# Neighbour codes before attention's set-up, and attention's end and statistics inside a selection, in a two-layer graph kernel

## What is computed

```python
# layer 0: h = relu(layernorm(x))
scores = where(A != 0, -arange(N), -inf)
vals, idx = top_k(scores, 25)              # the first 25 neighbours of each node
agg = X[idx].max(axis=2)                   # largest feature over them; relu of it if degree <= 25
x = x + relu(concat([X, agg]) @ W + b)
# layer 1: h = relu(layernorm(x))
hidden = h @ W.T
attn = leaky_relu(attn1[:, :, None] + attn2[:, None, :], 0.2)   # attn1, attn2 = hidden @ a
attn = softmax(where(mask > 0, attn, attn - 1e12))
x = x + attn @ hidden + bias
```

## Time and profile before

| what | value |
|---|---|
| runs, us | 5257.32, 5246.94, 5260.84 (median 5257.32) |
| profiled execution | 5242.94 us, its span 5241.1 us |
| POOL busy | 3058.9 us (58%), 3204 instructions |
| PE busy | 2621.3 us (50%) |
| DVE busy | 2599.8 us (50%) |
| ACT busy | 1563.8 us (30%) |
| granted TensorE clock, mean | 0.71 |

### The profile page before, as it was taken

The page is one execution under the profiler, slowest core; times in us unless marked ns, Lnnn a source line. Parts: engine busy times, 40 slices in busy tenths (PEclk is TensorE's granted clock), DMA queues, the critical chain, the costliest instruction groups (busy, mean ns, idle before and its releaser), DMA issues.

```text
span 5241.1 us, 38278 instructions
## 1 busy us (share of the span) xinstructions
PE 2621.3 (50%) x8782; PEld 1593.0 (30%) x8782; DVE 2599.8 (50%) x6725; ACT 1563.8 (30%) x1745; POOL 3058.9 (58%) x3204
## 2 busy tenths in 40 slices
PE   2122234556455555545555545555655555555479
PEld 1011112333233333323333323333323333332256
DVE  5444454455464455455445545445455554554442
ACT  3011122233332323333223333232333322333135
POOL 5565556566665666666666566665666665656520
PEclk8555557777676777666777767776766777766699
DMA  6354446556555566565555555656556665555320
GB/s 252 114 163 143 143 140 183 156 184 177 174 170 181 161 187 178 173 187 173 178 164 180 172 179 172 184 163 185 174 175 188 178 183 153 173 172 159 118 91 29
DMA packets 477228, 866.03 MB, mean 165 GB/s; under 512 B 308298, under 2 KB 309204, under 8 KB 456660
## 3 DMA queue, kind: packets, MB, share of 16 engines
q0 software_dynamic: 153600, 419.64, 27.8%
q1 hardware_dynamic: 305140, 378.64, 22.6%
q10 hardware_dynamic: 18432, 67.12, 3.5%
HBM read 690.98 MB, written 119.54 MB: 155 GB/s over the span
## 4 chain that ended last, share of the span: by engine, by line
PE 24%; DVE 23%; another core or an unknown queue 21%; issue 19%; ACT 10%; SPq 1%; DMA 1%; POOL 1%; ACTq 1%; DVEq 0%; POOLq 0%
PE acc L1331 13%; DVE highest L915 6%; ACT nm_t L566 4%; DVE lin L939 3%; DVE top L849 2%; DVE key L855 2%; PE bank L1264 2%; ACT wgt L602 2%; PE pen L1324 2%; PE pen L1323 1%; DVE stat L776 1%; PE bank L1244 1%; ACT pen L596 1%; POOL near L521 1%
## 5 line engine op out<-in xcount | busy, mean ns | idle before, releaser
L521 POOL DMA_INDIRECT near<-table_dram,idx x3200 | 3058.7, 956 | 1958.4 <-issue 990.5
L1331 PE MATMUL acc<-hid,wgt 128*128 (+1 forms) x4096 | 1163.2, 435 | 494.9 <-ACT wgt L602 431.4
L1331 PEld LDWEIGHTS acc<-hid,wgt 128*128 128x128 f32 x4096 | 873.6, 219 | 685.9 <-issue 427.4
L915 DVE TENSOR_TENSOR highest<-near,highest 128x512 f32<-128x512 f32 x1280 | 889.8, 695 | 142.6 <-DVE highest L915 65.2
L931 DVE SCALAR_TENSOR_TENSOR x_q<-bank,x_q 128x256 f32<-128x256 f32 x128 | 54.1, 423 | 1194.2 <-PE bank L1266 1038.3
L602 ACT ACTIVATE wgt<-pen,a_slope 128x512 f32<-128x512 f32 x448 | 304.7, 680 | 910.1 <-remote 576.3
L1264 PE MATMUL bank<-w_sb,h_t 128*128 128x256 f32 x1024 | 381.3, 537 | 334.1 <-ACT h_t L692 263.1
L566 ACT ACTIVATE nm_t<-adj_i,big_c 128x2048 bf16<-128x2048 int32 x128 | 498.0, 3941 | 4.9 <-DMA adj_i<-in_adj_dram 4.9
L1273 PE MATMUL acc<-cst,wgt 128*128 128x128 f32 x248 | 61.0, 427 | 812.1 <-ACT wgt L577 779.8
L939 DVE CUSTOM_DVE_ANT_0 lin<-acc,nm_q 128x2048 bf16<-128x2048 f32 x108 | 247.4, 2291 | 376.6 <-ACT acc L713 364.8
L849 DVE MAX8 top<-key 128x8 f32<-128x256 f32 (+1 forms) x1024 | 355.2, 386 | 127.6 <-remote 92.5
(11 more groups left out here) (148 smaller groups left out, 2172.4 us busy)
## 6 DMA issues: line engine op xcount, KB each, us to landing
adj_i<-in_adj_dram SPq DMA_DIRECT2D x128, 1024.0 KB
nmask_dram<-nm_t ACTq DMA_DIRECT2D x128, 512.0 KB
nm_q<-nmask_dram SPq DMA_DIRECT2D x29, 2048.0 KB
near<-table_dram,idx POOLq DMA_INDIRECT x3200
h_q<-table_dram SPq DMA_DIRECT2D x32, 512.0 KB
x_q<-in_x_dram SPq DMA_DIRECT2D x32, 512.0 KB
xmid_dram<-x_q SPq DMA_DIRECT2D x32, 512.0 KB
o_q<-xmid_dram SPq DMA_DIRECT2D x32, 512.0 KB
```

Source lines behind the costliest of these rows:

```text
L521: pool.indirect_dma_start(out=near[:, t % 2, k, :], out_offset=None, in_=table, in_offset=bass.IndirectOffsetOnAxis(ap=idx[:, t, k:k + 1], ...
L915: nc.vector.tensor_tensor(highest[:, :], pair(k), highest[:, :], ALU.max).then_inc(mx_step, 1)
L1331: mm = nc.tensor.matmul(acc[:, t, 0:C + 1], wgt_part(j)[:, t * P:(t + 1) * P], hid[:, bass.ds(batch * NJ + j, 1), 0:C + 1].rearrange("p a ...
```

## The change

It has two parts. In the first, PE packs the words of the next quad's first pair right behind layer 0 of tile 0, ahead of attention's set-up, and DVE makes the codes from them ahead of the maximum of tile 1. In the second, DVE's end of attention and the statistics stand between the two halves of the second pair's selection, behind the residual of tile 3, and no longer behind that selection.

```diff
--- before.py
+++ after.py
@@ -1154,7 +1154,6 @@
 
                 def selected(pair, between):
                     if "index" in stages:
-                        index_words(s + 1, pair)
                         index_rest(pair, between)
                     else:
                         between()
@@ -1162,11 +1161,20 @@
                 def third_tile():
                     finished(1)
                     gathered(2)
+
+                def quad_end():
+                    finished(3)
+                    if "attend" in stages:
+                        attend_end(a)
+                    if "gather" in stages:
+                        statistics_of_step(s, stages)
 
                 gathered(0)
                 if "attend" in stages:
                     attend_setup(a, lo)
                 finished(0)
+                if "index" in stages:
+                    index_words(s + 1, 0)
                 gathered(1)
                 selected(0, third_tile)
                 finished(2)
@@ -1174,13 +1182,9 @@
                     index_words(s + 1, 1)
                 gathered(3)
                 if "index" in stages:
-                    index_rest(1, lambda: finished(3))
+                    index_rest(1, quad_end)
                 else:
-                    finished(3)
-                if "attend" in stages:
-                    attend_end(a)
-                if "gather" in stages:
-                    statistics_of_step(s, stages)
+                    quad_end()
 
             b2.start(-1, -1)
 
@@ -1417,10 +1421,10 @@
                 if "project" in stages:
                     project(s - 1)
                 gathered(0)
+                if "index" in stages:
+                    index_prep(s + 1, 0)
                 if "attend" in stages:
                     attend_setup(a)
-                if "index" in stages:
-                    index_prep(s + 1, 0)
                 gathered(1)
                 for c in range(8):
                     if "attend" in stages:
```

## The result

| | before | after |
|---|---|---|
| median, us | 5252.13 (5237.10 to 5260.84, 4 runs) | 5336.70 (5323.85 to 5345.69, 4 runs) |
| profiled span, us | 5241.1 | 5340.6 |
| granted TensorE clock, mean | 0.71 | 0.70 |

The ratio is 1.0156, with a 95% interval of 1.0126 to 1.0186: 84.6 us slower. The forecast was 5345 in a range of 5180 to 5440.

The account below looks back on a forecast made before the run. Bound: one step's chain across engines, stretched by long POOL gather runs, not POOL alone. 3.0 us in 27 steps (81) plus 12 on 5242.94 gave 5336; plain runs' median is 14 us higher, so 5345, range 5180 to 5440.

Parts of the forecast that it names:

- Front half: Codes and index matmuls ahead of tile 1's maximum: a cost between 3.1 and 4.4 us a step, taken as 4.0.
- it ends at 2632.3, 4.4 us later: Tile 1's maximum starts 4.7 us later, falls wholly into POOL's slow stretch and so ends 4.4 us later.
- Two of my own signs: POOL's pause at `agg_made` near 9 us; forecast wrong if the second maximum ends less than 3 us later.
- a half sentence: Next POOL pauses end after POOL stops and carry its lateness on to the engines; reason for taking 4.0 us.
- Back half: Reciprocal and statistics right behind tile 3's residual: 4.7 us gained, less the front's 4.0; both branches still slower, 3.0 a step.
- the first branch: A hop (DVE to ACT or ACT to POOL) is held up and POOL stops at `h2_made`: 2.5 us slower.
- `project`'s start: If POOL stops at `h2_made`, `project` starts between 1 and 4 us later than before, taken as 2.5.
- L939's idle time: 13.3 us of cover for the moved rounds, used up if POOL passes `h2_made`; L939 then starts 3.5 us later.
- the steps without attention: Four steps where DVE waits for index matmuls held by ACT's masks: 0 to 9 us lost, 3 a step, 12 total.
- Codes late by 7.3 us: Rival: L1244's message to DVE is held up 7.3 us, 10.3 us a step lost, 5533 us; chance 0.14.
- The chain simply gets shorter: Rival: statistics end fast and the long run hurts nothing behind; 3.5 us a step faster, 5150 us; chance 0.24.
- Nothing measurable: Rival: front and back cancel (4.0 against 4.7), POOL's pauses absorb the rest; 5243 to 5270 us; chance 0.12.

Follow-up runs that it names:

- the kernel without pauses: Kernel before, with POOL's three waits at (1, 4), (1, 9) and (1, 21) left out: 5656.41 us, ratio 1.073.
- Part 1 alone: Kernel before plus only the words and codes moved ahead of attention's set-up, the statistics left behind the selection: 5345.31 us, ratio 1.0126.
- the early pause: POOL's wait for `out_made` moved from (1, 4) to (0, 23): changed kernel 5310.65 us, ratio 1.007; with only the second part of the change 5245.38 us, 0.996.
- the first trace: First profiled execution of the unchanged kernel, the one the prediction read: period 154.9 us, profiled span 5241.1 us.
- the control: Kernel before, unchanged, executed once more with the experiments: 5266.46 us, ratio 0.9995.
- part 2 alone: Kernel before plus only attention's end and statistics moved inside the second pair's selection: 5281.25 us, ratio 1.0009; with `out_made`'s wait also at (0, 23), 0.996.
- a second one: Changed kernel with `out_made`'s wait at (0, 23) and also the wait for tile 1's maximum moved from (2, 16) to (2, 18): 5220.62 us, ratio 0.9943.

## Why the prediction was right, and where it was off

**The mechanism.** That long POOL runs stretch what lies in them is shown: by two steps of one execution (7.9 against 19.5 us), by the kernel without pauses (32.8 us), and by moving one wait (L623 4.85 us behind its matmuls, then 0.15). Instructions themselves do not get longer, they start late: on DVE, operations of 0.17 us came 0.7 or 1.4 us apart inside the run and 0.2 us apart behind the stop; L623 started 5.2 us behind PE's matmuls. With half the bytes the held stretch was as long, so it is not the bytes. POOL's issuing or the number of gathers is left, and these runs don't part the two; nor do they show through what path it acts, or that DVE's late starts and ACT's have the same cause.

By the rule of the Trainium skill's page SBUF — State Buffer, section Who interferes with whom, only DVE's and GpSimd's shared port pair contends and PE and ACT are not slowed. L623, where PE hands over to ACT, was late by 5.2 us all the same, as L692 was by 7.3, so that rule does not account for them. DVE's own gaps it could allow, and no run here tests that.

That the change loses because it gives up the pause for `out_made` is not shown. Part 1 alone keeps that pause and the fast statistics and already loses 2.6 of the 3.1 us a step; the two executions of the kernel before have fast statistics in 4 and in 17 of 23 steps at nearly the same period. With the early pause part 1 costs much the same: 1.007 with it, 0.996 without.

**Front half: the term was 4.0 us and is 2.6 in time, of which 1.3 to 2.0 are there at the second maximum.** DVE's idle time before L867 was there (3.55 us), and so was PE's row scores' later start (18.3 us behind L939's start instead of 13.3). The step that failed is "it ends at 2632.3, 4.4 us later". The second maximum started 5.0 us later and ended 2.0 us later against the first trace, 1.3 against the control. I added the delay to a maximum whose duration I took from the first slow steps. But before, its end was itself held until 4 to 4.7 us behind POOL's stop (25.1, end 29.1 and 29.8), so most of the delay went into time that was already lost: the maximum shrank from 13.7 us to 10.7. Two of my own signs fail with it: the pause at `agg_made` is 6.3 us, here and in the mean, and not 9, and the maximum is less than 3 us later. I had listed the last as making the forecast wrong; it made only this term wrong.

**What then carries the lateness** is what I had as a half sentence. POOL resumes 0.8 us behind the second maximum, and both the gathers of tile 2 and the stop at (3, 8) follow by counting. A maximum of tile 2 that starts 2 us behind its last gather is 1.3 us later than the control's, the fourth L602 1.7 us. With part 1 alone L799 and `hid` are then 2.8 and 2.7 us later than the control's; where the last 1 us of it comes from stays open.

**Back half: the branch was right, its size too small.** POOL stopped for ACT's L577 (`h2_made`) in 23 of the steps, and missed it only among the last four, so this is the first branch. L1005 is behind the residual (0.30 us idle), and 4.4 us are off DVE's work (5.13 between their starts before, 0.72 after). For `project`'s start I took 2.5 us later; L799 ends 2.8 us later, and `hid` 3.4 us, as it is in turn held until POOL's next stop. Against the control, POOL's pauses at (1, 4) and (1, 9), 3.8 and 2.1 us in the median, became one of 7.6. L939's idle time shrank to 10 us, not to nothing, as the moved rounds took some 5 us in this branch. In time, part 2 gives nothing: 1.0009 by itself, and 0.5 us a step lost on top of part 1, which is within the intervals. The prediction had it give back 1.0 us of the front's 4.0.

**The sum.** I had 3.0 us in each of 27 steps and 12 us for the steps without attention, 93 in all. By the medians it is 3.1 us a step, and nothing in the others: there DVE does wait before the codes, for 6.68 us in one step, but the first L713 comes no later. (In the two profiled executions it is 3.9 us over 26 distances, 102.0, and the span grew by 99.5.) The 3.0 agrees with the 3.1 by luck in its parts: 4.0 less 1.0 was forecast, 2.6 and about 0.5 more were measured. What is left between 5345 and 5336.7 is mostly the 12 us that did not come. So 5345 was closer than its terms deserved.

**The rivals.** Codes late by 7.3 us: DVE's idle time was 3.55 us with 3.46 us of matmuls in it, so that message was in time. The chain simply gets shorter: by the runs that takes POOL's pause moved as well (part 2 alone 0.996), and for the whole change a second one (0.9943). Nothing measurable: true of part 2 alone (1.0009).

## What to carry to other kernels

Where one engine issues long trains of small transfers, ask of each step on the critical path where it lies in such a train and when the next pause comes. Shortening work that ends inside the train gave nothing here (1.0009) until the pause moved with it (0.996). And a wait of the issuing engine is not only a cost: taking three of them out made this kernel 7.3% slower, while moving two turned a loss of 1.6% into a gain of 0.6%. A faster stretch is not yet a faster step: the kernel before ran with fast statistics in 4 and in 17 of 23 steps, at periods of 154.9 and 155.8 us. When such a pause is moved, count the transfers left behind it, because the next tile waits for the last of them, and look whether the next pause is still there.

## What the hardware showed

- During unbroken runs of indirect gathers, issued 1.25 us apart, small instructions on DVE started 0.5 to 8.9 us after the one ahead of them had ended, where under 0.1 us is seen behind a pause. What was held started 2.4 to 4.7 us behind the stop.
- The held stretch stayed as long when each gather moved half the bytes (28.6 against 28.7 us for the same rounds).
- ACT's L623 started 0.04 us behind PE's matmuls 18 us into a run, 4.85 us (median) behind them in the changed kernel, where they ended 22 us into it, and 0.15 us (median) with POOL stopped.
- A pause of 2.4 us was enough to let a stretch of 8 us pass undisturbed, although it lay 12 to 20 us into the run that had started at 2257.56. In the other step shown, with no such pause, DVE's first late start came 15.7 us into the run.
